# Graph network kernel: TensorE runs unread matmuls of constants while it waits in the 8-head pass

## What is computed

```
q, k, v = feats @ Wq.T + bq, feats @ Wk.T + bk, feats @ Wv.T + bv      # (8 heads, nodes, 32)
sim  = sum over d of q[:, c] * k[:, r] / sqrt(32)                       # one number per edge and head
p    = exp(sim - segment_max(sim, c)[c])
attn = p / segment_sum(p, c)[c]
out  = segment_sum(attn * v[:, r], c) @ Wo.T + bo
```

## Time and profile before

| what | value |
|---|---|
| median of 3 runs | 6921.65 us (6920.33 to 6934.6) |
| profiled execution, own time | 6937.93 us |
| its span, first to last instruction | 6936.1 us |
| mean granted TensorE clock | 0.756 of full |
| 8-head pass, first to last L862 | 1498.3 to 2974.8 us |
| busy in 1498.3 to 2945.5 us | PE 1169.0, DVE 1210.0, ACT 1207.5, POOL 853.0 us of 1447.2 |

### The profile page before, as it was taken

The page is one execution under the profiler, slowest core; times in us unless marked ns, Lnnn a source line. Parts: engine busy times, 40 slices in busy tenths (PEclk is TensorE's granted clock), DMA queues, the critical chain, the costliest instruction groups (busy, mean ns, idle before and its releaser), DMA issues.

```text
span 6936.1 us, 96613 instructions
## 1 busy us (share of the span) xinstructions
PE 4636.9 (67%) x17264; PEld 3100.5 (45%) x17265; DVE 4381.6 (63%) x11395; ACT 2510.0 (36%) x7600; POOL 4659.8 (67%) x5272
## 2 busy tenths in 40 slices
PE   2555555978888878884766667567777775555555
PEld 1333333545555555563444444444444444433343
DVE  5555554668888888874666666556566664444546
ACT  0000000348888888855555555522222240000004
POOL 5777777355555555657777776677777737777772
PEclk6777777987777777796777777777777787777775
DMA  3333334367777777745444444344444543333334
GB/s 84 104 105 104 104 104 98 108 213 221 223 218 220 225 217 222 215 126 146 130 131 130 131 129 96 111 131 130 129 134 131 117 131 105 104 104 104 104 105 103
DMA packets 499183, 962.05 MB, mean 139 GB/s; under 512 B 105402, under 2 KB 296605, under 8 KB 491711
## 3 DMA queue, kind: packets, MB, share of 16 engines
q0 software_dynamic: 240064, 696.46, 37.3%
q1 hardware_dynamic: 258845, 263.03, 12.0%
HBM read 895.84 MB, written 64.63 MB: 138 GB/s over the span
## 4 chain that ended last, share of the span: by engine, by line
PE 37%; POOL 23%; issue 17%; DVE 14%; DVEq 4%; DMA 2%; ACT 1%; SPq 1%; POOLq 1%; ACTq 0%
POOL ring L711 23%; PE bank L1026 21%; DVE acc L1509 4%; PE bank L1074 3%; PE bank L1299 3%; DVE ring L1729 2%; DVE aux L1578 1%; DMA ring<-g_t,stage 1%; DVE acc L1506 1%; PE bank L1089 1%; DVEq L1751 1%; PE bank L1091 1%; PE bank L1090 1%; DVE ohc L1734 1%; PE bank L1235 1%
## 5 line engine op out<-in xcount | busy, mean ns | idle before, releaser
L1026 PE MATMUL bank<-ring,ohc 128*128 128x256 f32 (+3 forms) x8800 | 3243.3, 524 | 1652.8 <-DVE acc L1527 353.3
L1026 PEld LDWEIGHTS bank<-ring,ohc 128*128 128x128 f32 x8800 | 2104.0, 257 | 2572.0 <-DVE acc L1527 946.4
L711 POOL DMA_INDIRECT ring<-g_t,stage x1760 | 1734.4, 985 | 533.2 <-issue 469.8
L711 POOL DMA_INDIRECT ring<-kv_t,stage x880 | 855.4, 972 | 610.6 <-PE bank L1026 355.6
L1509 DVE TENSOR_TENSOR acc<-acc,bank 128x261 f32 (+1 forms) x1760 | 746.2, 424 | 576.2 <-PE bank L1026 480.4
L711 POOL DMA_INDIRECT ring<-in_x,stage x880 | 836.7, 951 | 266.1 <-issue 256.4
L711 POOL DMA_INDIRECT ring<-xs_t,stage x880 | 835.4, 949 | 260.8 <-issue 258.8
L1527 DVE TENSOR_TENSOR acc<-acc,bank 128x256 f32 x1760 | 736.7, 419 | 220.8 <-DVE acc L1527 204.2
L826 ACT ACTIVATE ring<-ring 128x32 f32<-128x32 f32 x3520 | 751.0, 306 | 0.0
L795 ACT ACTIVATE ohc<-iota,rel_c 128x128 f32<-128x128 f32 x1760 | 558.0, 388 | 70.9 <-PE bank L1026 68.7
L849 ACT ACTIVATE cl<-cl 128x1 f32<-128x1 f32 (+3 forms) x111 | 22.5, 203 | 1481.9 <-DVE mx L1722 1278.7
(11 more groups left out here) (310 smaller groups left out, 5425.7 us busy)
## 6 DMA issues: line engine op xcount, KB each, us to landing
aux<-relb_t SPq DMA_DIRECT2D x56, 1024.0 KB
aux<-q_t SPq DMA_DIRECT2D x880, 64.0 KB
relx<-relb_t SPq DMA_DIRECT2D x55, 512.0 KB
ring<-g_t,stage POOLq DMA_INDIRECT x1760, 2.8
x<-ring SPq DMA_DIRECT2D x21, 896.0 KB, 4.1
ring<-x SPq DMA_DIRECT2D x21, 896.0 KB, 9.2
mk<-mk SPq DMA_DIRECT2D x445, 32.1 KB
ring<-in_x,stage POOLq DMA_INDIRECT x880, 2.8
```

Of the source, the lines that this page charges most:

```text
L711: g_.indirect_dma_start(out=rings[L][:, slot, 0:W], out_offset=None, in_=table[L][:, :], in_offset=bass.IndirectOffsetOnAxis(ap=stage[:, s ...
L1026: return mm(banks[k % AB][:, 0:width], ohc[:, hot, :], rg[:, slot, vo:vo + width], start=True, stop=True)
```

## The change

In pass `L == 1` alone, the wait for `added` is moved ahead of the waits for `oc`, `wv` and `wa`, and behind it TensorE issues `FILL[k]` bfloat16 matmuls of 256 columns. Both operands are the identity matrix's bits read as bfloat16 (weights: its first 128 columns, moving: all 256), and they write the bank that sum k overwrites next; nothing reads them. FILL is 14 for sum 0, 0 for sums 1 to 3, 6 for sums 4 to 7 and 3 for sums 8 to 15: 62 in a batch.

```diff
+FILL = [14, 0, 0, 0] + 4 * [6] + 8 * [3]
@@
+                    filler = ident[:, :].bitcast(BF16)
+
+                    def fill(bank, count):
+
+                        for _ in range(count):
+                            mm(bank[:, 0:256], filler[:, 0:128], filler[:, :], start=True, stop=True)
+
                     def add_tiles(b, rset, k0, k1):
 
                         for k in range(k0, k1):
+                            free = 8 if L == 1 and k == 0 else 9 - AB
+                            if L == 1:
+                                pe.wait_ge(p["added"], b * G + (k + free + summed(L)))
+                                fill(banks[k % AB], FILL[k])
                             if k % 4 == 0:
...
                                 if L > 1:
                                     pe.wait_ge(p["wv"], b * (G // 4) + (weighed(L) + k // 4 + 1))
-                            free = 8 if L == 1 and k == 0 else 9 - AB
-                            pe.wait_ge(p["added"], b * G + (k + free + summed(L)))
+                            if L > 1:
+                                pe.wait_ge(p["added"], b * G + (k + free + summed(L)))
                             window_sum(rset * G + k, k % OHS, k).then_inc(p["agg"], 1)
```

## The result

The changed kernel takes 6767.2 us (median of 4 runs, 6760.49 to 6768.72) against 6923.51 (6920.33 to 6934.6) for the kernel before beside it: ratio 0.9765, 95% interval 0.9754 to 0.9777. Its profiled execution took 6768.2 us.

A forecast was written before the change was run, and what follows sets the result against it. TensorE's half clock was taken to bound the 8-head pass through VectorE's waits: 0.27 + 0.55 + 1.10 + 1.26 = 3.18 us a step, 53 x 3.2 = 169 us, so 6921.65 - 169 = 6752 us; range 6728 to 6845.

The forecast's parts named there:

- The clock: 8-head pass: fills keep TensorE at 2.4 GHz throughout; chance 0.70, 6752 us.
- The rival of a fall in part: 8-head pass: clock still falls once per batch for half of today's time; gain 85 us, 6837 us, chance 0.15.
- the slower one: Sums 8 to 15: unread, nearly all-zero matmuls do not keep the clock and only cost time; 7160 us, chance 0.05.
- the second half: Later part of a batch, where TensorE works without pause at half clock and pays for the clock lost earlier.
- The size: 8-head pass: step falls 3.18 us, from 27.31 to 24.1; 53 steps give 169 us.
- The listed waits: VectorE's waits for TensorE at L1578, L1652, L1506, L1620 and L1604: 3.88 us a batch, all a faster TensorE can give.
- own work and dependences: VectorE's part of a batch that a faster TensorE cannot shorten: 23.4 us of 27.31.
- The floor of ScalarE: ScalarE's loop without waits, 23.7 us a step; reached with no fills before sums 14 and 15, 6734 us.
- Sum 0: 14 fills, 1.5 us, hide in TensorE's 2.80 us standing still there; cost nothing, 0.8 us remain.
- Other loads: Same 16 gathers in a shorter step: DMA share rises from about 0.74 to 0.84, costing nothing to 0.5 us per batch.
- The loop of 771 instructions: TensorE's two-batch loop with fills may outgrow instruction memory and be refetched: 26 to 45 us lost, 6790 us, chance 0.05.
- the offset: Whole kernel: profiled execution lies 16.3 us above the median, taken to be the same after the change.

The follow-up runs named there:

- spread rows: Padding edges' source rows spread over the table instead of all row 0, on top of fills before sums 4 to 7 alone: 6693.28 us, ratio 0.9671 to the kernel before.

## Why the prediction was right

The forecast was 6752 us, the measurement 6767.2, inside the range. Step by step:

**The clock.** Full throughout, 1.00 instead of 0.75. That the fall starts between sums 4 and 8 is shown: 24 fills before sums 4 to 7, and none elsewhere, hold the level. The rival of a fall in part did not come, nor the slower one: matmuls of an identity do keep the clock. Whether a transpose would (the Trainium skill, "TensorE: Matmul & The Clock Gate", section on PE-mode transpose, says that it would not) no run here shows. The reading of the second half, that TensorE's work only pays there for what was lost in the first, was too simple: fills there alone took the time at half clock from 13.6 to 2.0 us a step and kept the clock up in half of the steps.

**The size.** 3.18 us were forecast for a step, 3.32 came. It is the sum of two errors against each other. The listed waits gave 3.88 - 1.08 = 2.80 us: L1652's wait was called gone and 0.40 us of it stays (20.3 / 51), the waits for sums 14 and 15 were called gone and 0.22 stays, and L1604's leaves 0.08; L1578's came out at 0.39 instead of 0.7. The other 0.52 us came from outside the list. VectorE's "own work and dependences", held fixed at 23.4 us, fell to 22.9, as here: first the kernel before, then the changed one.

```profile
1764.06 0.49 DVE L1506 SCALAR_TENSOR_TENSOR acc<-acc,aux,bank 128x264 f32 x1
...
1764.94 0.49 DVE L1506 SCALAR_TENSOR_TENSOR acc<-acc,aux,bank 128x264 f32 x1
...
1767.94 0.49 DVE L1506 SCALAR_TENSOR_TENSOR acc<-acc,aux,bank 128x264 f32 x1 [0.31 <-PE bank L1026]
...
1768.82 0.49 DVE L1506 SCALAR_TENSOR_TENSOR acc<-acc,aux,bank 128x264 f32 x1 [0.32 <-PE bank L1026]
```

```profile
1757.94 0.45 DVE L1518 SCALAR_TENSOR_TENSOR acc<-acc,aux,bank 128x264 f32 x1
...
1758.60 0.47 DVE L1518 SCALAR_TENSOR_TENSOR acc<-acc,aux,bank 128x264 f32 x1
...
1759.27 0.47 DVE L1518 SCALAR_TENSOR_TENSOR acc<-acc,aux,bank 128x264 f32 x1
```

Before, three of these additions come 0.88 us apart (the first starts at 1763.18, just ahead of the rows shown), after 0.66 and 0.67, with no wait printed at any. The pair at 1767.94 and 1768.82, where the wait for TensorE is printed, is 0.88 us apart as well, so I read the same wait, too short for the listing, in front of the others: 0.88 us is what a sum in a row costs at half clock. (The forecast's 0.955 us is a mean over four sums with what stands at their ends.) The two distances make 0.22 + 0.21 = 0.43 of the 0.52 us. The listed waits were taken for all that TensorE's clock could give, and they were not.

**The floor of ScalarE.** Put at 23.7 us and 6734 us, reached by having no fills before sums 14 and 15. Measured: 23.54 us and 6732.69. The times agree better than the working does: from the step and the number of steps stated, 3.6 x 53 is 191 us and not the 188 that were subtracted, the step gained 3.77 us and not 3.6, and the last two steps and the offset, below, took the rest back. That those two groups of fills (0.66 us of TensorE) lie on the path is shown with it: without them the step falls by 0.45 us, until ScalarE stops it.

**Sum 0.** The fills there cost nothing, as said, but 0.17 us of slack remained, not 0.8. They were not needed either, where the kernel before takes 6920 us.

**Other loads.** DMA share 0.82 where 0.84 was forecast, at no cost that shows in the step.

**The loop of 771 instructions.** It stays resident. The DMA queues of 1600 to 2740 us in the changed kernel are these two, and none of instruction fetches:

```profile
q0 software_dynamic: 60766, 199.14, 56.4%
q1 hardware_dynamic: 129193, 87.08, 25.8%
```

This agrees with the 2048 instructions that the Trainium skill, "Runtime: NRT & Kernel Launch", section on instruction fetch mechanics, gives PE.

**What failed: the last step and the offset.** Against its own profiled execution the forecast was 6769 us and 6768.2 came, but with two errors that cancel: 171.8 us from the regular steps, less 6.8 in the last two, which the prediction took as unchanged. They are set by the gathers of padding: with spread rows they take 23.46 us each instead of 31.06 and 28.90. Why they are longer in a faster pass than in the kernel before is not shown; that less of these gathers is done when a faster pass reaches them is my reading. What made the forecast of the median 15 us too low was the offset of 16.3 us between the profiled execution and the median, assumed to stay. The changed kernel's is 1.0 us. Before's profiled execution took 3762.2 us behind the gap after the pass, the changed kernel's 3754.8, where nothing was changed: about half of the offset was that one execution's own.

## What to carry to other kernels

Where the granted clock is below 1.00, find the stretch out of which it falls and try to fill that one alone, with unread work behind the wait that ends there: here 24 matmuls did all that 62 did, and the ones on the path cost what they take until another engine's loop becomes the bound. Work out that engine's loop without waits beforehand; it forecast the end of the gain to 0.2 us a step. Let padding point at different rows, and set the forecast from the medians, not from one profiled execution.

## What was not expected of the hardware

- Gathers that read one row for all 128 places kept the DMA engines busy for 0.80 of the time at 84 GB/s, against 0.35 at 105 GB/s for different rows.
- Fills behind the place where the clock falls help too: with three before each of sums 8 to 15 the time at half level in a step fell from 13.6 us to 2.0. In half of the steps the clock did not fall at all, with the same pauses of 0.81 us that it fell behind in others.
- On two of the chips engines stop at intervals for something that the profile calls "remote". Issues of gathers in the first pass, in the kernel without fills on such a chip, then VectorE's waits of that kind in 200 to 1200 us and the window of these 1000 us:

```profile
444.91 0.94 POOL L712 DMA_INDIRECT ring<-in_x,stage  x1 [0.31 <-issue]
449.67 0.95 POOL L712 DMA_INDIRECT ring<-in_x,stage  x1 [3.81 <-remote]
```

```profile
DVE ohc L1528 <- remote: 342.8, 45, 10.9
```

```profile
200.00:1200.00 1000.00, 467.93 (x1380) 335.12 (x1381) 463.80 (x1385) 0.00 (x0) 667.70 (x735) 0.72 0.32 91
```

The same window of the changed kernel on the chip where the kernel before takes 6920 us:

```profile
200.00:1200.00 1000.00, 571.41 (x1575) 393.69 (x1576) 533.40 (x1575) 0.00 (x0) 765.12 (x843) 0.76 0.38 103
```

A gather's issue takes 0.95 us on both, but 735 instructions of GpSimd instead of 843 fit, since it stands still for 3.7 to 4.1 us every 29 us (nine such intervals from 416 to 676 us, 28.9 on average). It is not GpSimd alone: between 445.9 and 448.9 us no engine starts an instruction, and VectorE waits 45 times for "remote" in these 1000 us. On the chips that take 6920 us no wait of GpSimd in this window is put down to it. The step of the 8-head pass is irregular there, 30.1 us without fills and 32.1 us with those before sums 4 to 7 and spread rows, although the granted clock over 1700 to 3300 us rises from 0.70 to 0.82. Why a higher clock goes with a longer step on those chips stays open: no experiment took the pauses and the clock apart, and the cause of the pauses is not in the traces.
